# Bias rows as three bf16 parts in one matmul, and row modulations made on two partitions and spread by DMA

## The reference

```
L0: h = ln(x); q = softmax(h Wq + bq), k = softmax over time, v = (h Wv + bv) * mask
    y = q (k^T v); x + silu(ln(y) (1 + scale) + shift) W_out + b_out
L1: shift, scale, gate = split(silu(c) W_ada + b_ada)
    h = ln(x) (1 + scale) + shift, permuted in time; x + gate * mamba(h)
L2: shift, scale, gate = split(silu(c) Wada^T + bada)
    skip = ln(x) (1 + scale) + shift; u = ln(skip)
    out = (silu(u Wx + bx) * (ssm1 + ssm2)) Wf + bf + skip; x + gate * out
L3: softmax attention with 16 heads, q, k, v with biases, then the modulated
    norm, silu, and the product with out_w, plus out_b, added to x
```

## Time and profile before

| | us |
|---|---|
| median of 3 runs | 2286.83 |
| lowest and highest | 2277.51 and 2296.69 |
| profiled execution, whole | 2285.24 |
| span of its profile | 2283.5 |
| TensorE busy (91% of the span) | 2088.7 |
| VectorE busy (71%) | 1615.9 |
| ScalarE busy (63%) | 1439.2 |
| gpsimd busy (46%) | 1059.5 |

### The profile page before, as it was taken

The page is one execution under the profiler, slowest core; times in us unless marked ns, Lnnn a source line. Parts: engine busy times, 40 slices in busy tenths (PEclk is TensorE's granted clock), DMA queues, the critical chain, the costliest instruction groups (busy, mean ns, idle before and its releaser), DMA issues.

```text
span 2283.5 us, 35035 instructions
## 1 busy us (share of the span) xinstructions
PE 2088.7 (91%) x13684; PEld 1450.4 (64%) x13684; DVE 1615.9 (71%) x2073; ACT 1439.2 (63%) x2422; POOL 1059.5 (46%) x589
## 2 busy tenths in 40 slices
PE   7996799987999899999999899899988999998997
PEld 4763499845998499849984799499853233232333
DVE  5444399735998399749984899499848877776621
ACT  3311599527994599659954897599642555554553
POOL 0003199712995289719960699099714000001000
PEclk9998799997999999979999999899999899998999
DMA  4012012111111112101110112011101111111000
GB/s 169 1 64 73 29 48 60 35 37 41 57 57 33 48 48 56 39 10 55 54 33 2 42 57 52 29 52 56 34 17 35 30 30 30 30 30 30 9 20 19
DMA packets 53738, 93.97 MB, mean 41 GB/s; under 512 B 11667, under 2 KB 20003, under 8 KB 52166
## 3 DMA queue, kind: packets, MB, share of 16 engines
q1 hardware_dynamic: 52038, 87.55, 12.9%
q0 software_dynamic: 1536, 4.20, 0.6%
HBM read 72.22 MB, written 6.89 MB: 35 GB/s over the span
## 4 chain that ended last, share of the span: by engine, by line
PE 67%; ACT 8%; issue 8%; DVE 8%; POOL 8%; DMA 0%; POOLq 0%; DVEq 0%; ACTq 0%; SPq 0%
PE PS L705 10%; PE PS L727 10%; POOL A L835 7%; PE PS L1384 6%; PE PS L257 5%; PE PS L1336 5%; PE PS L1522 5%; PE PS L710 5%; PE PS L247 4%; PE PS L590 2%; ACT A L790 2%; PE PS L255 2%; PE PS L733 2%; PE PS L1066 2%; ACT A L764 1%
## 5 line engine op out<-in xcount | busy, mean ns | idle before, releaser
L835 POOL TENSOR_TENSOR A<-A 128x1024 f32<-128x1024 f32 x384 | 897.9, 2388 | 156.8 <-ACT small L779 144.8
L790 ACT ACTIVATE A<-A,negA 128x512 f32<-128x512 f32 x768 | 552.1, 719 | 42.0 <-DVE A L823 32.6
L823 DVE TENSOR_TENSOR_SCAN A<-A,PS 128x512 f32<-128x512 f32 x384 | 434.5, 1200 | 55.1 <-ACT A L790 35.6
L823 DVE TENSOR_TENSOR_SCAN A<-A,small,PS 128x512 f32<-128x512 f32 x384 | 455.3, 1260 | 6.0 <-PE PS L705 5.5
L727 PE MATMUL PS<-ident,A 128*128 128x128 f32 x3072 | 402.2, 274 | 18.8 <-POOL A L835 13.8
L1558 ACT ACTIVATE A<-PS 128x1024 f32<-128x1024 f32 x256 | 262.4, 1025 | 225.3 <-PE PS L1522 223.7
L705 PE MATMUL PS<-A 128*128 128x128 f32 x3072 | 394.0, 281 | 7.1 <-DVE A L823 7.1
L1349 DVE TENSOR_REDUCE A<-PS 128x1 f32<-128x512 f32 x512 | 330.0, 686 | 87.0 <-PE PS L1336 84.4
L705 PEld LDWEIGHTS PS<-A 128*128 128x128 f32 x3072 | 373.8, 197 | 14.9 <-DVE A L823 9.3
L727 PEld LDWEIGHTS PS<-ident,A 128*128 128x128 f32 x3072 | 347.4, 141 | 28.9 <-POOL A L835 19.0
L764 ACT ACTIVATE A<-A,small 128x512 f32<-128x512 f32 x340 | 242.3, 717 | 24.2 <-PE PS L710 20.1
(11 more groups left out here) (202 smaller groups left out, 2144.4 us busy)
## 6 DMA issues: line engine op xcount, KB each, us to landing
A<-scrc SPq DMA_DIRECT2D x192, 256.0 KB, 3.2
A<-A SPq DMA_DIRECT2D x360, 32.0 KB
scr<-A SPq DMA_DIRECT2D x4, 1024.0 KB, 4.6
W<-in_wa SPq DMA_DIRECT2D x2, 1536.0 KB, 16.4
X<-in_x SPq DMA_DIRECT2D x4, 512.0 KB, 5.5
out<-X SPq DMA_DIRECT2D x2, 1024.0 KB, 4.5
W<-in_w SPq DMA_DIRECT2D x1, 1984.0 KB, 7.7
W<-in_wzc SPq DMA_DIRECT2D x1, 1536.0 KB, 11.0
```

Source lines behind the costliest of these rows:

```text
L790: e.activation(A_B[i % 4], r.DT[:, dt, ci * 512:(ci + 1) * 512], ACT.Exp, scale=negA[:, r.n, dt * 16 + s:dt * 16 + s + 1]).then_inc(*decay ...
L823: e.tensor_tensor_scan(h, a, u, init, ALU.mult, ALU.add).then_inc(*scanned.up((q, i)))
L835: e.tensor_tensor(h, h, CB[k % 2].unsqueeze(1).broadcast_to([128, 2, 512]), ALU.mult).then_inc(*weighed.up((q, pair)))
```

## The change

The bias rows no longer lie in fp32 on partitions 0, 32 and 64. They come as a tile RB of 16 x 128. gpsimd splits it into three bf16 parts: the rounded value, the rounded rest, and the rest of that. The parts go through DRAM into `ROW3`, three rows of 2048 bf16. One bf16 matmul with K = 3 and three rows of ones opens the accumulation in place of the fp32 one with K = 1. The parts are made ahead of the first norm's power in gpsimd's stream. In sync's stream the wait for them, three stores, a wait for these and the load of ROW3 stand ahead of the `wada` loads.

Row modulations are made once for both batches: the staying operand is silu(c) with its two columns, the result has two partitions. VectorE adds biases and combines with norm1's g and b on two partitions (`row_mods_v`); sync stores the 2 x 1024 result to DRAM and loads each batch's row back broadcast to 128 partitions, into `MODS`, which holds gate1, G2, H2 and gate2. This stands in sync's queue behind w1 and wzc, ahead of the stores at L381. VectorE waits for `MODS` where it first reads it. After each scan the ring of banks is set to bank 4, with marks for the last banks the scan used.

```diff
+        def bias_t(e, o, name):
+            a, n = ROWS[name]
+            e.matmul(o, ones3[0:3, :], ROW3[0:3, a:a + n], start=True, stop=False)
...
-                    p = 0 if bias.start_partition() == 0 else 32
-                    e.matmul(o[:, j * 256:(j + 1) * 256], ones[p:p + 1, :], bias, start=True, stop=False)
+                    bias_t(e, o[:, j * 256:(j + 1) * 256], bias)
...
+        def row_parts_p(e, w):
+            w.wait_ge(*transfer("rows").at(0))
+            for p in range(2):
+                w.wait_ge(*pool.now())
+                e.tensor_copy(RP[p], RB).then_inc(*pool.up())
+                w.wait_ge(*pool.now())
+                e.tensor_tensor(RP[2] if p else RB, RB, RP[p], ALU.subtract).then_inc(*pool.up("row_parts"))
...
-        def row_mod_t(e, w, key, wt, o, n, b, bias):
-            dst = take(w, key)[:, 0:n]
-            p = 0 if bias.start_partition() == 0 else 32
-            e.matmul(dst, ones[p:p + 1, :], bias, start=True, stop=False)
-            for k in range(4):
-                t = e.matmul(dst, sc[:, k, b:b + 1].broadcast_to([128, 128]), wt[:, k, o:o + n], start=False, stop=k == 3)
-            t.then_inc(*pe.up(key))
+        def row_mods_t(e, w):
+            o = take(w, ("rows", 0))
+            for k in range(4):
+                e.matmul(o[0:2, 0:256], sc[:, k, :], wada[1][:, k, 512:768], start=k == 0, stop=k == 3)
+            for k in range(4):
+                t = e.matmul(o[0:2, 256:512], sc[:, k, :], wada[2][:, k, 512:768], start=k == 0, stop=k == 3)
+            t.then_inc(*pe.up(("rows", 0)))
+            o = take(w, ("rows", 1))
+            for k in range(4):
+                t = e.matmul(o[0:2, :], sc[:, k, :], wada[2][:, k, 0:512], start=k == 0, stop=k == 3)
+            t.then_inc(*pe.up(("rows", 1)))
+
+        def row_mods_v(e, w):
+            w.wait_ge(*transfer("row_mods").at(0))
+            w.wait_ge(*pe.at(("rows", 0)))
+            o = bank(("rows", 0))
+            e.tensor_tensor(MW[:, 0:256], o[0:2, 0:256], WR[:, 0:256], ALU.add).then_inc(*dve.up())
+            e.tensor_tensor(MW[:, 768:1024], o[0:2, 256:512], WR[:, 768:1024], ALU.add).then_inc(*dve.up())
+            banks.give(("rows", 0), dve.now())
+            w.wait_ge(*pe.at(("rows", 1)))
+            e.tensor_tensor(WR[:, 256:768], bank(("rows", 1))[0:2, :], WR[:, 256:768], ALU.add).then_inc(*dve.up())
+            banks.give(("rows", 1), dve.now())
+            w.wait_ge(*dve.now())
+            for g in range(2):
+                e.scalar_tensor_tensor(out=MW[:, 256 * (g + 1):256 * (g + 2)], in0=WR[:, 512:768], scalar=1.0, in1=WR[:, 1024 + 256 * g:1280 + 256 * g],
+                                       op0=ALU.add, op1=ALU.mult).then_inc(*dve.up())
+            w.wait_ge(*dve.now())
+            e.tensor_tensor(MW[:, 512:768], MW[:, 512:768], WR[:, 256:512], ALU.add).then_inc(*dve.up("row_mods"))
...
-            e.dma_start(ROW[0:1, :], T["rows0"]).then_inc(*transfer("row0").up(0))
-            e.dma_start(ROW[32:33, :], T["rows1"]).then_inc(*transfer("row1").up(0))
-            e.dma_start(ROW[64:65, 0:512], T["rows2"]).then_inc(*transfer("row2").up(0))
+            e.dma_start(RB, T["rows"]).then_inc(*transfer("rows").up(0))
...
+            w.wait_ge(*pool.at("row_parts"))
+            for p in range(3):
+                e.dma_start(scrb[p].rearrange("(i s) -> i s", s=128), RP[p]).then_inc(*transfer("row_parts").up(0))
+            w.wait_ge(*transfer("row_parts").at(0))
+            e.dma_start(ROW3[0:3, :], scrb).then_inc(*transfer("row3").up(0))
+            e.dma_start(WR, T["row_mods"].partition_broadcast(2)).then_inc(*transfer("row_mods").up(0))
...
+            w.wait_ge(*dve.at("row_mods"))
+            e.dma_start(scrm, MW).then_inc(*transfer("mods_out").up(0))
+            w.wait_ge(*transfer("mods_out").at(0))
+            for b in range(NB):
+                e.dma_start(MODS[:, b, :], scrm[b].partition_broadcast(128)).then_inc(*transfer(f"mods{b}").up(0))
...
+            e.memset(ones3[:, :], 1.0).then_inc(*pool.up())
...
+            row_parts_p(e, w)
             for b in range(NB):
                 norm_p(e, w, ("ln0", b), range(b * TB, (b + 1) * TB))
...
+            banks.at, banks.held = 4, [[("last y", q, j)] for j in range(4)] + [[("last u", q, j)] for j in range(4)]
...
+            for j in range(4):
+                banks.give(("last y", q, j), taken.at((q, r.order[1], j)))
+                banks.give(("last u", q, j), scanned.at((q, UNITS - 4 + j)))
...
+                w.wait_ge(*transfer(f"mods{b}").at(0))
...
-                e.matmul(o, ones[64:65, :], ROW[64:65, 0:512], start=True, stop=False)
+                bias_t(e, o, "l2bx")
```

More of the change, by code:

```diff
@@ L103 @@
     NCOL += _n
[L104 to L106 removed]
+ROWS = {"l0bq": (0, 256), "l0bv": (256, 256), "l0bo": (512, 256), "l2bf": (768, 256), "l3bv": (1024, 256), "l3bo": (1280, 256), "l2bx": (1536, 512)}
+NROW = 2048
 def program(nc, T, out):
@@ L121, in program @@
         COL = sb("COL", [128, NCOL])
-        ROW = sb("ROW", [128, NROW])
+        ROW3 = sb("ROW3", [128, NROW], BF16)
+        ones3 = sb("ones3", [128, 128], BF16)
         ident = sb("ident", [128, 128])
@@ L134, in program @@
         MT = sb("MT", [128, 4, 2])
[L135 to L138, removed]
+        MODS = sb("MODS", [128, 2, 4 * D])
+        gate1, G2, H2, gate2 = (MODS[:, :, D * j:D * (j + 1)] for j in range(4))
         negA = sb("negA", [128, 3, 64])
@@ L148, in program @@
         scrc = [nc.dram_tensor(f"scrc_{q}", (NS, S), F32, kind="Internal").ap() for q in range(6)]
+        scrb = nc.dram_tensor("scrb", (3, NROW), BF16, kind="Internal").ap()
+        scrm = nc.dram_tensor("scrm", (NB, 4 * D), F32, kind="Internal").ap()
         scr4 = nc.dram_tensor("scr4", (3, NB * S), BF16, kind="Internal").ap()
@@ L161, in transfer @@
             return dma[name]
-        for name in (["x0", "x1", "x2", "x3", "cols", "row0", "row1", "row2", "idx", "w0", "mask", "wa0", "wa1", "wa2", "wa3", "w1", "wzc0",
+        for name in (["x0", "x1", "x2", "x3", "cols", "rows", "row_parts", "row3", "row_mods", "mods_out", "mods0", "mods1", "idx", "w0", "mask", "wa0", "wa1", "wa2", "wa3", "w1", "wzc0",
                       "wzc1", "w2", "wf", "w3", "maskf", "mask_rows", "max_out0", "max_out1"]
@@ new lines, in program @@
+        RP = [area(31360 + 64 * p, 64).bitcast(BF16)[0:16, :] for p in range(3)]
+        WR = area(31616, 1536)[0:2, :]
+        MW = area(33152, 1024)[0:2, :]
+        def row_parts_p(e, w):
[5 more added lines that the diff above has]
+                e.tensor_tensor(RP[2] if p else RB, RB, RP[p], ALU.subtract).then_inc(*pool.up("row_parts"))
@@ L308, in modulations_t @@
             column_mods_t(e, w, 2, wada[3])
[L309 to L315, removed]
+            row_mods_t(e, w)
         def modulations_v(e, w):
@@ L319, in modulations_v @@
             column_mods_v(e, w, 2, "l3be", "l3w2", "l3b2")
[L320 to L336, removed]
+            row_mods_v(e, w)
             w.wait_ge(*act.at("exp_a"))
@@ L405, in first_t @@
                         project_t(e, w, ("k", b, h, c), lambda k, m: W0k[:, k, m * 128:(m + 1) * 128], 2, h, lambda k: XN[:, k, c * 512:(c + 1) * 512])
[L406 to L408 removed]
+            w.wait_ge(*transfer("row3").at(0))
             for i in range(0, NT, 2):
[L410 to L411 removed]
+                tokens_t(e, w, ("v", i), lambda k, i: XN[:, k, i * 128:(i + 1) * 128], 2, lambda k: W0v[:, k, :], "l0bv", (i, i + 1))
+                tokens_t(e, w, ("q", i), lambda k, i: XN[:, k, i * 128:(i + 1) * 128], 2, lambda k: W0q[:, k, :], "l0bq", (i, i + 1))
                 o = take(w, ("ek", i))
@@ L448, in first_t @@
                 w.wait_ge(*act.at(("sn0", i // 4, 1)))
-                tokens_t(e, w, ("o0", i), lambda k, i: SN0[:, k, i * 128:(i + 1) * 128], 2, lambda k: W0o[:, k, :], row0("l0bo"), (i, i + 1))
+                tokens_t(e, w, ("o0", i), lambda k, i: SN0[:, k, i * 128:(i + 1) * 128], 2, lambda k: W0o[:, k, :], "l0bo", (i, i + 1))
         def first_s(e, w):
@@ L1101, in layer2_t @@
                     w.wait_ge(*act.at((("yt2", b), 1, 3)))
-                    tokens_t(e, w, ("o2", b, j), lambda k, i: YD2[:, k, i * 128:(i + 1) * 128], 4, lambda k: Wf[:, k, :], row1("l2bf"), (j, j + 1))
+                    tokens_t(e, w, ("o2", b, j), lambda k, i: YD2[:, k, i * 128:(i + 1) * 128], 4, lambda k: Wf[:, k, :], "l2bf", (j, j + 1))
         def layer2_s(e, w):
@@ L1213, in front_t @@
                 w.wait_ge(*act.at((("xn3", job // TB), job // 4, 1)))
-                e.matmul(o, ones[0:1, :], row0("l3bv"), start=True, stop=False)
+                bias_t(e, o, "l3bv")
                 for k in range(2):
@@ L1426, in tail_t @@
                 w.wait_ge(*act.at((("sn3", b), i // 4, 1)))
-                tokens_t(e, w, ("o3", i), lambda k, i: SN[b][k][i // 4 % 2][:, i % 4 * 128:(i % 4 + 1) * 128], 2, lambda k: Wo[:, k, :], row0("l3bo"),
```

(7 more changed lines are left out.)

9 lines of the change are left out of this document (2 added, 7 removed).

## The result

| | before | changed |
|---|---|---|
| median, us | 2282.72 (4 runs, 2277.51 to 2296.69) | 2219.88 (4 runs, 2214.85 to 2225.14) |
| profiled execution's span, us | 2283.5 | 2215.7 |
| ratio of the times | | 0.9716, 95% interval 0.9663 to 0.9768 |

The changed kernel is faster by 62.8 us in the medians; the spans of the two profiles stand 67.8 us apart. The forecast was 61.3 off the profiled execution, and 2226 for the median.

The account below looks back on a forecast made before the run. TensorE was taken as the bound, with 67% of the chain's span. Biases 50.8 plus row modulations 13.6 minus start 3.1 gave 61.3 us off 2285.24, 2223.9, or 2226 for the median; range 2208 to 2246, chance 0.76.

Parts of the forecast that it names:

- The price of the bias: New bias piece on TensorE: 0.21 us for 256 columns, 0.32 for 512, saving 0.41 and 0.73 us each.
- switch price stays: Rival: the switch at each bias keeps its price, 0.30 and 0.42 us a bias, 2237 us; chance 0.11.
- The load pulled ahead: At the bias switches: the skill's rule would hide the load, 11 us more; set aside because the rows disagree.
- v/q loop, o2, values: Biases in the v/q loop, o2 and layer 3's values, all on the path: gains 13.1, 6.6 and 6.6 us.
- o0: 16 biases of o0 in layer 0: VectorE becomes the bound by half a microsecond; gain 6.2 us.
- Row modulations: Layer 0, both batches in one pass: 9.7 us instead of 23.3, gain 13.6 us, bounds 8.4 to 15.8.
- Start: gpsimd waits for the rows and splits them before the first power: 11.75 instead of 8.66, cost 3.1 us.
- Sync's queue: Sync's added stores, waits and spreading stay hidden; store1 free by some 3 us in the transfers.
- Gates: `gates_t`, 2 x 8 biases of 512 columns on the chain: 16 x 0.73 = 11.7 us.
- Last stage: Eight o3 biases that end the kernel: the stage takes 10 instead of 13.5 us, gain 3.3.
- Engines that take over: Rival: another engine bounds gates, o2, values and o3, which give nothing (31.5 us), 2257 us; chance 0.10.
- The clock rival: Rival: TensorE gets 1.2 GHz in the stretches that now hold biases, 182 us on top, 2408 us; chance 0.03.

Follow-up runs that it names:

- rows_128: The changed kernel with the bias matmul over 128 rows instead of 3, zeros below the three parts; 2183.86 us, 0.9555 of before.
- parts_late: The changed kernel with the splitting of the rows moved behind the power of the first batch's norm on gpsimd; 2214.65 us, 0.9667 of before.
- after_again: The changed kernel profiled once more, nothing changed; 18.4 us from the first product of batch 0's gates to the start of the last.

## Why the prediction was right

**The price of the bias** was right to the digit: 0.21 and 0.32 us, as read off the score matmul that follows a matmul of another kind. There was luck in the choice of that row: what it follows has 128 rows too and differs in its columns (32 in the operand that stays), so it is a switch of another sort that happens to cost the same 0.10. That the exposed part is a load, which shrinks with the type, was the choice between 0.19 and 0.10, and it held: 0.09 us of load in the source view. What it lacked was the reason for the exposure; that lay in the number of rows, and with it some 26 of the 36 us that `rows_128` was faster. "A load does not start under the matmuls of the other kind" was too wide a reading of the earlier trace rows: the 99-row bf16 matmul behind an fp32 product shows none of its load (1740.14). The rival "switch price stays" falls.

**The load pulled ahead.** With 3 and 64 rows the loads stay in the chain, with 128 they lie under the product before. The Trainium skill (TensorE: Matmul & The Clock Gate, the steps of a matmul) has a load pulled ahead of matmuls in flight if the row groups don't conflict or it goes to the background weight buffer; the prediction set that aside for this switch, rightly: with 3 and 64 rows next to 128 the loads weren't pulled ahead. Where 128 or 99 rows stand next to 128 they were, and there the traces agree with the page.

**v/q loop, o2, values:** 13.2, 6.7 and 3.3 us (batch 0) against 13.1, 6.6 and 3.3. The counts and the slack of VectorE were enough. The values of batch 1 gave 2.9 against 3.3, for one of their eight biases lies behind VectorE.

**o0:** 6.5 against 6.2. VectorE did become the bound at the end: four adds in a row without a wait.

**Row modulations:** 14.8 against 13.6. The working had the clock return in the middle of gate2; it returned before it (1.73 us, full clock). In `parts_late`, `rows_128` and `after_again` it returned in the middle, and gate2 took 2.14 to 2.32 us and the whole 9.1 to 9.3, so 0.6 to 0.8 us of the excess is the clock of this execution. The exposed load of 0.19 is gone too (1.73 instead of 1.92, 3.43 instead of 3.62), because no bias with K = 1 stands ahead of the products any more. The two columns aren't the reason: eight instructions of o2 with 128 output columns also take 1.73 in `rows_128`, where they took 1.92 in both kernels.

```profile
1131.67 1.73 PE PS L253 x8
```

**Start:** first power 2.9 us later (forecast 3.1), first bias 2.6.

**Sync's queue:** hidden, as forecast. Spreading issued at 135.1 and landing in 4.8 us, store1 wanted at 146.9: 7 us of slack instead of the 3 worked out.

**Gates:** the mis-sized term. Forecast 11.7 for both batches, measured 18.4, all of the 6.7 us too much in batch 0. The step that failed is the 16 x 0.73: it priced all gates at full clock, though the earlier trace rows has three of them at half clock with a bias of 2.00 us, which became 0.54. With the same three gates slow, batch 0 would have given 3 x 1.46 + 5 x 0.73 = 8.0 us instead of 5.8 (an estimate from these pieces), so 2.2 of the 6.7 us were there to be read. The other 4.5 are the clock: two of the three slow gates ran at full clock, and this came again in every profile of the changed kernel and of its variants with 3 or 64 rows. The split depends on what is held fixed. Had the low clock lasted as long into the shorter gates as before, 17.1 us, batch 0 would have given only 6.0, and nearly all of the 6.7 would be the clock's.

**Last stage:** 2.2 against 3.3, for its first product ran at half clock (2.00 us for 1.06) in this execution.

**The sum** was 61.3, against 67.8 in the profiled executions and 62.8 in the medians. The profiles' excess of 6.5 is the gates' 6.7; the row modulations' 1.2, the start's 0.5 and o0's 0.3 were offset by the last stage (-1.1), the stretch ahead of the row modulations (-0.8) and the values of batch 1 (-0.4). That the medians came within 1.5 us is partly luck: single runs of one kernel lie 10 to 19 us apart.

**Engines that take over** did so only within o0, by half a microsecond; in the gates of batch 0 VectorE's du (from 954.7 to 963.4) now ends 1.2 us before them (964.6), so that little more could be gained there. The clock rival, as the case that ends slower, fell: the mean granted clock went from 0.946 to 0.949.

## What to carry to other kernels

A short matmul over few rows, put between matmuls over 128, costs its neighbour nearly as much as itself (0.19 us beside 0.21): padding its operands with zeros to 128 rows took 0.30 us off each bias of 256 columns, and the source line of the bias had shown none of the 0.19 us that lay in the product behind it. When a piece of a chain is 0.2 us longer than its streaming, ask at each end whether the weight load could run under the matmul before it. Work made ready for later (here the split rows) should stand in an engine's stream behind the first thing that the path waits for.

## What the runs showed of the hardware that was not expected

- A matmul over 3 rows and one over 64 cost the same at a switch to and from 128 rows: 0.10 us for the bf16 load and 0.19 for the fp32 load. Over 128 rows neither shows, nor does that of a bf16 matmul over 99 rows behind one over 128, and the fp32 load of 0.19 stays out of the chain although the bias before it streams only 0.11 us. The timeline has that load start with the bias (40.77 and 40.76) and the product at 40.87; how the whole of it fits in there isn't shown.
- Two and 128 output columns stream equally long (eight instructions of 256 columns: 1.73 us in the new row modulations, and 1.73 in the o2 products of `rows_128`).
- TensorE stayed at 1.2 GHz for some 27 us while it was busy all the time (granted clock 0.51 from 966 to 994 in the kernel before), the last 17 of them in gates with K = 1 fp32 biases. With 3-row bf16 biases the low stretch lasted some 14 us (0.69 from 934 to 936, 0.50 to 948, 0.79 from 948 to 949), and the clock was back 3 us into the gates. The slow gates came alike in four profiles with the one kind of bias and in two of the changed kernel. Here are the two stretches of the kernel before, in the order of the earlier trace rows:

```profile
966.00:994.00 28.00, 28.00 (x39) 9.57 (x37) 15.56 (x11) 16.91 (x18) 4.74 (x1) 0.51 0.00 0
994.00:1009.00 15.00, 15.00 (x33) 5.15 (x33) 1.24 (x1) 1.20 (x2) 0.00 (x0) 1.00 0.00 0
```

- Fp32 column modulations (two moving columns) lasted from 8.7 to 11.5 us for the same 64 instructions in different profiles, by the granted clock: 8.8 x 0.79 and 11.5 x 0.59 are both some 6.9 us.
